# Second experts of an audio tower: routing in three groups instead of two, a new order of the stage, and the last chunk in halves

## The chip, the cores and the metric

The kernel runs on one core of a Trainium2 chip. The engines are TensorE (PE: matrix products and transposes; its weight loads are shown as PEld), VectorE (DVE), ScalarE (ACT), GpSimd (POOL) and SyncE (SP, which here issues transfers). Each works off its own list of instructions in the order written, and they wait for one another with semaphores. The metric is the device time of one execution in microseconds (us).

## The reference, cut to what matters

Sixteen signals are turned into 16 x 255 tokens of 64 numbers. Two blocks of attention and experts follow, each added to its input after a normalisation over the 64 numbers. The change is in the last step, the second layer of experts. Each token's eight router logits choose two of eight experts, with a softmax over the two:

```python
def _moe(tokens, router_w, w1, b1, w2, b2):
    logits = tokens @ router_w.T
    probs = jax.nn.softmax(logits, axis=-1)
    rw, re = jax.lax.top_k(probs, 2)
    rw = rw / jnp.maximum(rw.sum(-1, keepdims=True), 1e-12)
    combine = zeros((N, E)).at[arange(N)[:, None], re].set(rw)
    out = tokens
    for e in range(8):
        h = gelu(tokens @ w1[e] + b1[e])     # 64 -> 64, the exact gelu
        y = h @ w2[e] + b2[e]                # 64 -> 64
        out = out + combine[:, e:e + 1] * y
    return out

h = h + attention1(layernorm(h))
h = h + _moe(layernorm(h), ...)              # what this text is about
```

All experts are computed for all tokens, and the weights, zero for six of eight, are applied to the hidden values.

## The kernel before

The 32 tiles of 128 tokens are worked on in 8 chunks of 4 tiles (CH, TC); 16 signals make two tiles each. The last stage begins while the second attention is still finishing its last signals: `slot(B // 2, k, ...)` and `slot(B // 2 + 1, k, ...)` are those remnants, and on DVE they hold the reading of the turned outputs (slot 3, L2176 to L2187), the last addition of the projected outputs Y (slot 7, L2187, semaphore `s_fin`), and the normalisation of the last signals (L447 to L455 on DVE, the root L460 on POOL, the scaling L472 on DVE).

For a chunk c the stage does this, in columns of 512 tokens:

- PE turns the normalised tokens (`x_turn`, L1821), and ACT copies them out (`columns_out`, L2067).
- PE multiplies with the router (`logits`, L1837); DVE copies the logits (`logits_out`, L2266) and finds the two best (`rank`, L2271 and L2274).
- For 16 tiles at once, DVE takes the difference of the two best (`difference`, L2279 and L2280), ACT its exponential (`gap`, L2072), and DVE builds the weights of the eight experts, split into three bf16 parts (`combine`, L2285 to L2304).
- PE turns these weights (`weights`, L1847), and ACT copies them out (L2076).
- For each of two groups g of four experts: PE's `hidden(c, g)` (L1861), ACT's gelu (L2097), PE's `spread(c, g)` of the weights over the rows (L1874), DVE's `weigh(c, g)` (L2322), PE's `second(c, g)` (L1884, with the bias L1889 where g is 0).
- ACT copies the chunk's sum (`y_out`, L2082), PE turns it (`sum_turn`, L1899), and DVE adds its two halves to the tokens (`finish`, L2312 and L2313). POOL has added the normalised tokens to them before (`add_x`, L2458). SP stores the chunk with four transfers, in a loop over the chunks (`store`, L2476).

Each engine's order is written out by hand. The work shares PE's eight result banks: the hidden values have banks 0 to 3, the spread weights 4 and 5, the sums bank 6, the turned sums bank 7; tokens, logits and turned weights borrow banks between. Bank 6 also holds the attention's projected outputs Y. A reader must be done with a bank before the next result is written there, and most of the waits say that. `keep_clock` is a filler: products of constants that nobody reads. On ACT, Exp and Gelu lie in different tables, so that a `gap` between two gelus costs a load of each (ACT_TABLE_LOAD).

DVE's `combine(n)` works on half of the tiles (`half`), and it stands behind `best(0)` to `best(3)` for the first half and between two weighings of chunk 2 for the second.

Of the kernel before, what the change touches and what calls it, by code (L numbers as in the profile page):

```python
# [25 lines left out]
P = 128  # L26
# [61 lines left out]
def tower(nc, x, taps, consts, w_raw, gate_b0, w1_01, b1_0, w2_0, b2_0, gamma,  # L88
          split_sel, wpos, wproj, bproj, b1_1, w2_1, b2_1, out):
    with ExitStack() as ctx:  # L90
# [1379 lines left out]
        def attention1_and_experts1(block, e0):  # L1470
# [66 lines left out]
            half = NT // 2  # L1537
# [7 lines left out]
            wgt = [mo[:, 2048 + 512 * n:2560 + 512 * n] for n in range(4)]  # L1545
            y_sb = mo[:, 4096:4608]
            yy = mo[:, 4608:4864].rearrange("p (t d) -> p t d", t=TC)
            GROUPS = 2
            X_BANK, WEIGHT_BANK = (0, 1, 0, 1, 7, 7, 7, 7), (7, 6, 4, 5)
            LOGIT_BANK = (2, 4, 2, 4, 4, 4)  # L1550
            def logit_tile(c, k):
                bank, column = (LOGIT_BANK[c] + k % 2, k // 2) if c < 6 else (7, k)
                return ps[:, bank, E * column:E * column + E]

            def logit_tiles(c):
                if c < 6:
                    both = ps[:, LOGIT_BANK[c]:LOGIT_BANK[c] + 2, 0:TC // 2 * E]
                    return both.rearrange("p n (t e) -> p t n e", t=TC // 2)[:, :, :, 0:E]
                return ps[:, 7, 0:TC * E].rearrange("p (t n e) -> p t n e", n=2, t=TC // 2)[:, :, :, 0:E]

            H1, CB, Y1, YT = (lambda g, n: ps[:, 2 * g + n]), (lambda n: ps[:, 4 + n]), ps[:, 6], ps[:, 7]
            turned_weights = lambda d: ps[0:96, WEIGHT_BANK[d // 2], 256 * (d % 2):256 * (d % 2) + 256].bitcast(BF16)
# [12 lines left out]
            def _(pe):  # L1575
# [230 lines left out]
                def x_turn(c):  # L1806
# [3 lines left out]
                    elif c < 4:  # L1810
                        pe.wait_ge(s_xc, c - 1)
                    elif c == 4:
                        pe.wait_ge(s_otr, B)
                    elif c == 5:
                        pe.wait_ge(s_xc, 5)
                    elif c == 6:
                        pe.wait_ge(s_ct, 2)
                    else:
                        pe.wait_ge(s_lc, c)
# [4 lines left out]
                def logits(c):  # L1824
                    pe.wait_ge(s_xc, c + 1)
                    if c == 0:
                        pe.wait_ge(s_E, UNITS)
                    elif c == 1:
                        pe.wait_ge(s_O, QUADS * B)
                        pe.wait_ge(s_k, UNITS)  # L1830
                    elif c < 4:
                        pe.wait_ge(s_lc, c - 1)
                    elif c < 6:
                        pe.wait_ge(s_lc, c)
                    for k in range(TC):
                        rows = head(k % 2) if c < 6 else head(0)
# [3 lines left out]
                def weights(d):  # L1840
                    pe.wait_ge(s_c3, d // 4 + 1)
                    if d == 0:
                        pe.wait_ge(s_xc, 6)
                    elif d == 1:
                        pe.wait_ge(s_ct, 1)
# [4 lines left out]
                def hidden(c, g):  # L1850

                    s = GROUPS * c + g
                    if s == 0:
                        pe.wait_ge(s_xc, 4)
                    elif s == 1:
                        pe.wait_ge(s_lc, 3)
                    else:
                        pe.wait_ge(s_hid, s - 1)
# [5 lines left out]
                def spread(c, g):  # L1864

                    s = GROUPS * c + g
                    pe.wait_ge(s_ct, 1 if s < 2 else 4 if s < 7 else CH)
                    if s == 0:
                        pe.wait_ge(s_lc, 6)
                    if s >= 1:  # L1870
# [6 lines left out]
                def second(c, g):  # L1877

                    s = GROUPS * c + g
                    if g == 0 and c >= 1:  # L1880
                        pe.wait_ge(s_ysb, c)
                    pe.wait_ge(s_wgt, s + 1)
                    for n in range(2):
# [8 lines left out]
                def sum_turn(c):  # L1892
# [3 lines left out]
                    else:  # L1896
                        pe.wait_ge(s_lc, CH)
                    for k in range(TC):
# [7 lines left out]
                slot(B // 2, 3, ("tail",))  # L1906
                x_turn(2)
                logits(1)
                x_turn(3)
                logits(2)  # L1910
                logits(3)
                hidden(0, 0)
                slot(B // 2, 6, ("tail",))
                x_turn(4)
                hidden(0, 1)
                logits(4)
                x_turn(5)
                slot(B // 2, 7, ("tail",))
                pe.wait_ge(s_lc, 5)
                keep_clock(5, 2)  # L1920
                logits(5)
                weights(0)
# [672 lines left out]
```

## Time and profile before

| | before |
|---|---|
| median of 3 runs | 729.52 us (726.92 to 729.8) |
| the profiled execution | 728.98 us |
| its span, first to last instruction | 727.2 us |
| PE, DVE, ACT, POOL busy in the span | 87%, 79%, 69%, 48% |
| mean granted clock of PE | 0.968 of 2.4 GHz |

The span is what the trace shows; the execution's own time has 1.78 us around it. Views used below: the chain of waits (the work that ended last, followed back step by step), the timeline of an engine (instructions in order of time, neighbours of one kind merged), the windows (busy time of each engine in a stretch, with the granted clock), the figures of one line, and the issues of transfers. Times of day are microseconds from the start of the span. A matrix product's shown duration is longer than the distance to the next one, since they overlap in the array.

### The profile page before, as it was taken

The numbers are of one execution on the slowest core, as the hardware profiler recorded it, in microseconds if no ns is written. First come the engines' busy times: TensorE is split into PE (matmuls) and PEld (weight loads), VectorE is DVE, ScalarE is ACT, GpSimd is POOL, SyncE is SP. The second block draws the span as 40 slices with busy tenths as digits, with TensorE's granted clock in tenths as the row PEclk, the third lists the DMA queues.
The fourth block names the chain that finished last, engine by engine and source line by source line (L and its number), as shares of the span: only waits on it lengthen the run. The fifth ranks groups of instructions, "written<-read, shape, count | busy, mean of one in ns | idle before, by whom it ended". The sixth has DMA issues, their size and how long they took to land.

```text
span 727.2 us, 16349 instructions
## 1 busy us (share of the span) xinstructions
PE 631.7 (87%) x4940; PEld 347.4 (48%) x4940; DVE 571.1 (79%) x1627; ACT 501.2 (69%) x1264; POOL 351.6 (48%) x440
## 2 busy tenths in 40 slices
PE   5548998999999997999999998699898889877895
PEld 4534665566666664222222225355565555554331
DVE  6676786777777776789999989659888888959753
ACT  2746875888888874567777777648777777755552
POOL 1006577778878775523444444725354555423000
PEclk9858999999999999999999999799999999998999
DMA  4030000000000000633333330000000000000011
GB/s 112 1 116 1 1 3 0 0 0 0 0 0 0 0 1 3 205 118 119 117 117 114 108 117 16 2 0 2 2 1 0 0 0 0 1 1 1 11 23 27
DMA packets 22422, 24.37 MB, mean 34 GB/s; under 512 B 12390, under 2 KB 13414, under 8 KB 22118
## 3 DMA queue, kind: packets, MB, share of 16 engines
q1 hardware_dynamic: 20135, 23.31, 10.3%
q10 hardware_dynamic: 2239, 0.49, 0.3%
q8 instruction: 22, 0.36, 0.2%
q14 instruction: 26, 0.21, 0.1%
HBM read 22.48 MB, written 1.31 MB: 33 GB/s over the span
## 4 chain that ended last, share of the span: by engine, by line
PE 51%; DVE 25%; issue 9%; ACT 3%; POOL 2%; DMA 2%; SPq 0%; DVEq 0%; POOLq 0%; ACTq 0%
PE ps L726 8%; PE ps L762 8%; DVE big L1110 6%; PE ps L1591 5%; PE ps L1613 4%; PE ps L720 4%; DVE big L2130 3%; DVE big L1151 3%; PE ps L1597 2%; DVE big L1060 2%; PE ps L712 2%; PE ps L1884 2%; PE ps L708 2%; PE ps L1861 2%; PE ps L1728 1%
## 5 line engine op out<-in xcount | busy, mean ns | idle before, releaser
L1367 POOL TENSOR_TENSOR big<-big 128x1024 f32<-128x1024 f32 x64 | 119.8, 1893 | 47.0 <-DVE big L1171 47.0
L949 ACT ACTIVATE big<-ps,big 128x255 f32<-128x255 f32 x256 | 117.0, 483 | 10.0 <-DVE big L1165 7.5
L911 ACT ACTIVATE big<-ps,b1s 128x512 f32<-128x512 f32 x128 | 80.7, 682 | 29.4 <-PE ps L644 28.3
L1165 DVE TENSOR_REDUCE big<-ps 128x4 f32<-128x1020 f32 x64 | 75.1, 1213 | 26.0 <-PE ps L720 26.0
L1988 ACT ACTIVATE big<-ps 128x1024 f32<-128x1024 f32 x64 | 65.9, 1030 | 33.1 <-PE ps L1603 30.8
L726 PE MATMUL ps<-cst,big 128*128 128x128 f32 x512 | 78.3, 287 | 7.0 <-POOL big L1367 3.0
L2130 DVE TENSOR_REDUCE big<-ps 128x4 f32<-128x1020 f32 x64 | 78.1, 1220 | 6.8 <-DVE res L2187 2.5
L1177 DVE COPY mid<-ps 128x512 f32<-128x512 f32 x96 | 63.5, 686 | 19.0 <-PE ps L726 15.7
L726 PEld LDWEIGHTS ps<-cst,big 128*128 128x128 f32 x512 | 55.5, 143 | 41.5 <-issue 20.8
L644 PE MATMUL ps<-big,wall 64*128 64x512 f32 x256 | 72.1, 640 | 0.4 <-ACT big L882 0.4
L655 PE MATMUL ps<-big,w2s 128*64 128x512 f32 x256 | 69.0, 616 | 2.6 <-DVE big L1151 2.2
L762 PE MATMUL ps<-mid,big 128*64 128x256 f32 (+1 forms) x512 | 69.9, 393 | 0.0
L1151 DVE SCALAR_TENSOR_TENSOR big<-ps,b2s,mid 128x512 f32<-128x512 f32 x64 | 48.0, 749 | 10.3 <-DMA mid<-spread_w 6.8
L949 ACT ACTIVATION_READ_ACCUMULATOR big<-ps,big 128x1 f32 x256 | 55.6, 217 | 0.0
L1591 PE MATMUL ps<-big,selqk 128*128 128x256 bf16 x384 | 52.8, 273 | 0.7 <-ACT big L1964 0.4
L465 POOL TENSOR_TENSOR big<-big 128x4 f32<-128x4 f32 x16 | 16.4, 1028 | 65.0 <-DVE big L455 64.9
L1110 DVE TENSOR_TENSOR big<-big 128x512 f32<-128x512 f32 x56 | 47.1, 841 | 0.0
L937 ACT ACTIVATE big<-ps 128x512 f32<-128x512 f32 x64 | 34.9, 602 | 12.6 <-PE ps L708 10.4
L460 POOL TENSOR_TENSOR mid<-mid 128x2 f32<-128x2 f32 x16 | 11.5, 716 | 61.7 <-DVE mid L455 61.7
L1591 PEld LDWEIGHTS ps<-big,selqk 128*128 128x128 bf16 x384 | 32.7, 97 | 17.1 <-issue 13.5
L1597 PE MATMUL ps<-big 64*128 64x256 bf16 x256 | 25.4, 273 | 17.8 <-DVE big L2130 17.7
L762 PEld LDWEIGHTS ps<-mid,big 128*64 128x64 f32 (+1 forms) x512 | 31.3, 137 | 19.0 <-issue 8.4
(282 smaller groups left out, 1317.7 us busy)
## 6 DMA issues: line engine op xcount, KB each, us to landing
mid<-spread_w SPq DMA_DIRECT2D x128, 128.0 KB, 2.8
mid<-in_split_sel SPq DMA_DIRECT2D x1, 1536.0 KB, 7.5
wall<-in_w SPq DMA_DIRECT2D x1, 1280.0 KB, 6.7
out_tokens<-res SPq DMA_DIRECT2D x16, 56.0 KB, 1.6
cst<-in_consts SPq DMA_DIRECT2D x1, 520.5 KB, 5.0
pexp<-in_w_raw SPq DMA_DIRECT2D x1, 512.0 KB, 5.5
w2s<-in_w SPq DMA_DIRECT2D x1, 512.0 KB, 3.3
mid<-in_taps ACTq DMA_DIRECT2D x1, 320.0 KB, 3.9
```

The lines of the kernel that those rows point to most:

```text
L644: last = nc.tensor.matmul(H1(e, j), wst[0][half, f:f + P], xc[q][half], start=True, stop=True)
L655: last = nc.tensor.matmul(Y(e)[D * j:D * j + D], w2s[0][:, 2 * e + j], hid[e % 2][j], start=True, stop=True)
L726: last = nc.tensor.transpose(AT[:, j, c, P * tq:P * tq + P], e_sb[r % 4][:, j, tq, P * c:P * c + P], ident)
L762: last = nc.tensor.matmul(O[D * j:D * j + D, par], val[par][0:n, c, D * h:D * h + D], a_sb[r % 4][0:n, j, c], start=(g == 0 and a == 0 and ...
L911: last = nc.scalar.activation(hid[e % 2][j], H1(e, j), ACT.Relu, bias=b1s[0][:, 2 * e + j:2 * e + j + 1])
L949: last = nc.scalar.activation(e_sb[r % 4][:, jj, tq, 0:NW], S[:, 2 * (r % 2) + jj, tq, 0:NW], ACT.Exp, scale=-1.0, bias=minus[r % 4][:, jj ...
L1110: ins = nc.vector.tensor_tensor(acc[q], acc[q], part[e % 2], ALU.add)
L1151: nc.vector.scalar_tensor_tensor(out=acc[q] if e == 0 else part[e % 2], in0=Y(e), scalar=b2s[:, e:e + 1], in1=cb[e % RING], op0=ALU.add, o ...
L1165: nc.vector.tensor_reduce(minus[r % 4], S[:, 2 * a:2 * a + 2, :, 0:NW], AX.X, ALU.min).then_inc(s_mx, 1)
L1367: nc.gpsimd.tensor_tensor(e_sb[r % 4], e_sb[r % 4], bc(inverse[r % 4].unsqueeze(3), [P, 2, 2, 256]), ALU.mult).then_inc(s_A, 1)
L1591: last = nc.tensor.matmul(out_, selqk[:, 2 * p + n, part], parts[par][:, part], start=(part == 0), stop=(part == 2))
L2130: nc.vector.tensor_reduce(mx[k % 2], S[:, :, :, 0:NW], AX.X, ALU.max).then_inc(s_max, 1)
```

## The change

The diff, with the waits shortened to those that the text speaks of. The routing groups are now chunk 0, chunks 1 to 3 and chunks 4 to 7 (`ROUTED`), the logits are copied for chunk 0, chunks 1 to 3, 4 and 5, 6 and 7 (`LOGITS_READ`). Results lie in other banks. POOL adds the tokens of chunk c only when the sum of chunk c - 1 is turned. In the last chunk the second product, `y_out`, the turn and `finish` are done for each of the two signals; SP issues four of its stores, after its loop, and ACT four.

```diff
-            half = NT // 2
-            X_BANK, WEIGHT_BANK = (0, 1, 0, 1, 7, 7, 7, 7), (7, 6, 4, 5)
-            LOGIT_BANK = (2, 4, 2, 4, 4, 4)
+            ROUTED = ((0, 1), (1, 4), (4, CH))
+            LOGITS_READ = ((0, 1), (1, 4), (4, 6), (6, CH))
+            X_BANK, WEIGHT_BANK = (0, 1, 4, 5, 7, 7, 7, 7), (4, 7, 6, 6, 7, 7, 7, 7)
+            YL, YTL = (ps[:, 6, 0:256], ps[:, 0, 0:256]), (ps[:, 7, 0:256], ps[:, 1, 0:256])
...
                 def logits(c):
-                    pe.wait_ge(s_xc, c + 1)
+                    pe.wait_ge(s_xc, c + 1 if c < 4 else c // 2 * 2 + 2)
-                        rows = head(k % 2) if c < 6 else head(0)
+                        rows = head(k % 2) if c < 4 else head(0)
...
                 def weights(d):
-                    pe.wait_ge(s_c3, d // 4 + 1)
+                    pe.wait_ge(s_c3, 1 if d == 0 else 2 if d < 4 else 3)
...
+                    elif d == 4:
+                        pe.wait_ge(s_done, 2)
+                    elif d == 6:
+                        pe.wait_ge(s_ct, 6)
+                        pe.wait_ge(s_done, 3)
...
                 def second(c, g):
+                    if s == 0:
+                        pe.wait_ge(s_fin, B)
+                    elif g == 0:
                         pe.wait_ge(s_ysb, c)
+                    if s == GROUPS:
+                        pe.wait_ge(s_ct, 4)
                     pe.wait_ge(s_wgt, s + 1)
+                    if c == CH - 1:
+                        for b in range(2):
+                            for n in range(2):
+                                last = nc.tensor.matmul(YL[b][D * n:D * n + D], w2s[1][:, 2 * g + n], wgt[2 * g + n][:, 256 * b:256 * b + 256], start=(g == 0), stop=(g == GROUPS - 1))
...
                 def sum_turn(c):
...
+                    elif c == 2:
+                        pe.wait_ge(s_ct, 6)
+                    elif c == 3:
+                        pe.wait_ge(s_ct, CH)
...
 # PE, from slot(B // 2, 3) on
-                x_turn(2); logits(1); x_turn(3); logits(2); logits(3)
-                hidden(0, 0); slot(B // 2, 6, ("tail",)); x_turn(4)
-                hidden(0, 1); logits(4); x_turn(5)
-                slot(B // 2, 7, ("tail",))
-                pe.wait_ge(s_lc, 5); keep_clock(5, 2)
-                logits(5); weights(0)
-                for c in range(CH): ...     # as printed above
+                logits(1); x_turn(2); x_turn(3); hidden(0, 0)
+                logits(2); logits(3); weights(0); hidden(0, 1); spread(0, 0)
+                slot(B // 2, 6, ("tail",)); x_turn(4); hidden(1, 0)
+                slot(B // 2, 7, ("tail",)); spread(0, 1); second(0, 0)
+                x_turn(5); hidden(1, 1); logits(4); logits(5); second(0, 1)
+                pe.wait_ge(s_wgt, 2); keep_clock(4, 3)
+                for d in range(1, 4): weights(d)
+                spread(1, 0); hidden(2, 0); sum_turn(0); spread(1, 1)
+                second(1, 0); hidden(2, 1); x_turn(6); spread(2, 0)
+                second(1, 1); x_turn(7); hidden(3, 0); logits(6); logits(7)
+                spread(2, 1); sum_turn(1); second(2, 0)
+                for c in range(3, CH):
+                    hidden(c, 1); spread(c, 0); second(c - 1, 1)
+                    if c < CH - 1: hidden(c + 1, 0)
+                    spread(c, 1)
+                    if c < 5:
+                        second(c, 0)
+                        for d in (4, 5) if c == 3 else (6, 7): weights(d)
+                        sum_turn(c - 1)
+                    else:
+                        sum_turn(c - 1); second(c, 0)
+                second(CH - 1, 1)
+                for b in range(2): ...      # the two halves of the last sum turned
 # ACT
+                columns_out(0); columns_out(1); gap(0); columns_out(2); columns_out(3)
+                gelu(0, 0); weights(0); gelu(0, 1); slot(B // 2, 6, ())
+                columns_out(4); gelu(1, 0); columns_out(5); gap(1); y_out(0); gelu(1, 1)
+                for d in range(1, 4): weights(d)
+                gelu(2, 0); gelu(2, 1); columns_out(6); y_out(1); columns_out(7)
+                gelu(3, 0); gap(2); y_out(2); gelu(3, 1); weights(4); weights(5)
+                gelu(4, 0); y_out(3); gelu(4, 1); weights(6); weights(7)
+                for c in range(5, CH): gelu(c, 0); y_out(c - 1); gelu(c, 1)
...
+                    for first, n in ((0, 112), (112, 15)):
+                        nc.scalar.dma_start(out[2 * CH - 2 + b, P + first:P + first + n], res[first:first + n, 4 * CH - 4 + 2 * b + 1]).then_inc(s_out, 16)
 # DVE, from slot(B // 2, 1) on
+                logits_out(0); rank(0); difference(0); combine(0)
+                logits_out(1); slot(B // 2, 3, ()); rank(1); weigh(0, 0)
+                rank(2); rank(3); difference(1); slot(B // 2, 7, ()); weigh(0, 1)
+                logits_out(2); combine(1); slot(B // 2, 2, ()); slot(B // 2, 5, ())
+                slot(B // 2, 6, ()); slot(B // 2 + 1, 1, ()); weigh(1, 0)
+                slot(B // 2 + 1, 2, ()); finish(0); rank(4); weigh(1, 1)
+                rank(5); weigh(2, 0); logits_out(3); weigh(2, 1); finish(1)
+                rank(6); rank(7); difference(2); weigh(3, 0); combine(2)
+                weigh(3, 1); finish(2)
+                for c in range(4, CH): weigh(c, 0); weigh(c, 1); finish(c - 1)
+                for b in range(2): ...      # finish of the two halves
 # POOL
-                for c in range(CH - 2): add_x(c)
+                pool.wait_ge(s_c3, 1); add_x(0)
                 norm.root(pool, B - 2); norm.root(pool, B - 1)
-                for c in range(CH - 2, CH): add_x(c)
+                for c in range(1, CH):
+                    pool.wait_ge(s_yt, c); add_x(c)
 # SP
-                with sp.Fori(0, CH) as c:
+                with sp.Fori(0, CH - 1) as c:
                     store(c)
+                for b in range(2):
+                    sp.wait_ge(s_done, CH + b)
+                    for first, n in ((0, 112), (112, 16)):
+                        sp.dma_start(out[2 * CH - 2 + b, first:first + n], res[first:first + n, 4 * CH - 4 + 2 * b]).then_inc(s_out, 16)
```

In `combine` the first comparison and the first product no longer wait for their own end before the next instruction.

## Rows read from the trace of the kernel before

**Rows 1.** The chain of waits: start, us, what.

```profile
656.06 0.20 DVE mid L2266
...
657.37 0.20 DVE mid L2266
...
667.77 2.01 PE ps L1861 x4
...
672.89 0.79 PE ps L1837 x8
...
695.71 1.06 PE ps L1861 x4
696.76 0.32 PE ps L1874 x2
```

**Rows 2.** Timeline of PE: start, us, what, idle time before and what ended it.

```profile
651.07 0.61 PE L1837 MATMUL ps<-gates,big 64*128 64x8 f32 x8 [0.25 <-ACT big L2067]
...
701.11 1.13 PE L1861 MATMUL ps<-big,wall 64*128 64x512 f32 x4
...
706.59 1.13 PE L1861 MATMUL ps<-big,wall 64*128 64x512 f32 x4
...
717.69 1.08 PE L1884 MATMUL ps<-big,w2s 128*64 128x512 f32 x4 [0.56 <-DVE big L2322]
```

**Rows 3.** Windows: stretch, length, busy of PE, PEld, DVE, ACT, POOL, PE's clock, DMA.

```profile
663.00:666.40 3.40, 1.49 (x12) 0.75 (x11) 2.88 (x14) 1.21 (x3) 0.19 (x1) 0.50 0.00 0
685.00:687.00 2.00, 0.28 (x4) 0.26 (x4) 1.82 (x6) 1.99 (x4) 0.00 (x0) 1.00 0.00 0
694.00:705.20 11.20, 11.20 (x55) 3.69 (x56) 6.65 (x12) 6.33 (x12) 0.00 (x0) 1.00 0.12 25
```

**Rows 4.** Timeline of DVE.

```profile
655.03 0.26 DVE L2176 RECIPROCAL big<-ps 128x16 f32<-128x16 f32 x1
...
664.66 0.60 DVE L472 TENSOR_SCALAR big<-res,mid 128x128 f32<-128x128 f32 x2
...
665.97 0.16 DVE L455 TENSOR_TENSOR mid<-mid 128x2 f32<-128x2 f32 x1
666.44 1.29 DVE L2322 TENSOR_TENSOR big<-big,ps 128x512 f32<-128x512 f32 x2 [0.31 <-PE ps L1874]
...
682.28 0.61 DVE L2285 TENSOR_TENSOR mid<-cst,mid 128x128 f32<-128x128 f32 x2
684.22 0.17 DVE L2290 TENSOR_SCALAR mid<-mid 128x16 f32<-128x16 f32 x1 [1.32 <-ACT mid L2072]
...
687.02 0.56 DVE L2304 TENSOR_TENSOR mid<-mid 128x384 bf16<-128x384 f32 x1
```

**Rows 5.** Timeline of POOL.

```profile
656.32 4.14 POOL L2458 TENSOR_TENSOR res<-res,big 128x256 f32<-128x256 f32 x6
666.21 0.71 POOL L460 TENSOR_TENSOR mid<-mid 128x2 f32<-128x2 f32 x1 [5.75 <-DVE mid L455]
```

**Rows 6.** Timeline of ACT and of the transfers that it issues (ACTq).

```profile
1.91 1.84 ACTq L229 DMA_DIRECT2D mid<-in_x  x1
...
676.12 2.42 ACT L2097 ACTIVATE big<-ps,b1s 128x512 f32<-128x512 f32 x4
...
682.61 1.28 ACT L2072 ACT_TABLE_LOAD   x1
683.90 0.22 ACT L2072 ACTIVATE mid<-mid 128x16 f32<-128x16 f32 x1
```

**Rows 7.** Line 2280: count, shortest, median and longest in ns, first and last start.

```profile
L2280 DVE CAST mid<-mid x2: 173/462/751, 659.1 to 678.9; 128x32 f32<-128x32 uint32 x2
```

**Rows 8.** Timeline of the transfers that SP issues.

```profile
44.90 0.90 SPq L1442 DMA_DIRECT2D w2s<-in_w  x2
...
721.31 2.43 SPq L2476 DMA_DIRECT2D out_tokens<-res  x4
```

**Rows 9.** Line 2476, the stores, in the form of rows 7.

```profile
L2476 SPq DMA_DIRECT2D out_tokens<-res x32: 322/332/1232, 681.4 to 724.1; - x32
```

More of the change, by code:

```diff
@@ new lines, in _ @@
+                pe.wait_ge(s_wgt, 2)
+                keep_clock(4, 3)
+                for d in range(1, 4):
+                    weights(d)
+                spread(1, 0)
+                hidden(2, 0)
+                sum_turn(0)
+                spread(1, 1)
+                second(1, 0)
+                hidden(2, 1)
+                x_turn(6)
+                spread(2, 0)
+                second(1, 1)
+                x_turn(7)
+                hidden(3, 0)
+                logits(6)
+                logits(7)
@@ L2115, in _ @@
-                y_out(CH - 1)
+                gelu(1, 0)
+                columns_out(5)
+                gap(1)
+                y_out(0)
+                gelu(1, 1)
+                for d in range(1, 4):
+                    weights(d)
+                gelu(2, 0)
+                gelu(2, 1)
+                columns_out(6)
+                y_out(1)
+                columns_out(7)
+                gelu(3, 0)
+                gap(2)
+                y_out(2)
+                gelu(3, 1)
+                for d in (4, 5):
+                    weights(d)
@@ new lines, in _ @@
+                gelu(4, 0)
+                y_out(3)
+                gelu(4, 1)
+                for d in (6, 7):
+                    weights(d)
+                for c in range(5, CH):
+                    gelu(c, 0)
+                    y_out(c - 1)
+                    gelu(c, 1)
+                act.wait_ge(s_yt, CH - 1)
+                for b in range(2):
+                    act.wait_ge(s_w2, GROUPS * CH + b)
+                    nc.scalar.activation(y_sb[:, 256 * b:256 * b + 256], YL[b], ACT.Copy).then_inc(s_ysb, 1)
@@ L2345, in _ @@
+                slot(B // 2 + 1, 2, ())
+                finish(0)
                 rank(4)
[L2346 to L2347 removed]
+                weigh(1, 1)
                 rank(5)
[L2349 to L2355 removed]
+                weigh(2, 0)
+                logits_out(3)
+                weigh(2, 1)
@@ L2356, in _ @@
+                finish(1)
+                rank(6)
+                rank(7)
+                difference(2)
+                weigh(3, 0)
+                combine(2)
+                weigh(3, 1)
+                finish(2)
+                for c in range(4, CH):
                     weigh(c, 0)
-                    if c == 2:
-                        combine(1)
                     weigh(c, 1)
                     finish(c - 1)
-                finish(CH - 1)
+                dve.wait_ge(s_with_x, CH)
```

252 lines of the change are left out of this document (124 added, 128 removed).

## Prediction

> **What bounds the kernel now.** I read the page first: TensorE (PE) is busy for 87% of the span, VectorE (DVE) for 79%, ScalarE (ACT) for 69%. The change touches only the last tenth, from 650 us on, so I then read the chain of waits there and the timelines beside it. Up to 664 us the chain runs on DVE: copies of logits, ranking, and the routing weights of 16 tiles built at once [rows 1, 4]. From 694 on it runs on PE: from the second hidden product of chunk 5 to that of chunk 6 it takes 706.59 - 701.11 = 5.48 us, and of the 11.2 us from 694.0 PE is busy for 11.20 [rows 2, 3]. Between them PE waits for weights, tables and weighed tiles, and from 663.0 its granted clock is 0.50 (1.2 GHz), after waits that left it busy for 1.49 of 3.4 us [rows 3]. In the tail, PE's last second product starts at 717.69, the last store is issued at 724.1, and the span ends at 727.2 [rows 2, 9].
>
> With PE saturated from chunk 4 on, the change gains only if PE waits less before that, or in the tail.
>
> **The change, by a walk through the new orders.** I lay each engine's new order down with the durations of these rows, from the end of the first logits (651.07 + 0.61 = 651.7), which nothing new precedes [rows 2].
>
> *Prices.* DVE: logits copy and ranking of a chunk 657.37 - 656.06 = 1.31, the copy 0.23 of it; the reading of the attention's last outputs (slot 3) 656.06 - 655.03 = 1.03 [rows 1, 4]. Weighing two tiles 1.28, of which the next instruction overlaps 0.08; scaling a pair of tiles and the statistics of the next 665.97 + 0.16 - 664.66 = 1.47, POOL's root between them 0.71 [rows 4, 5]. A finish has two instructions over half of a weigh's elements, 0.8. A combine of 16 tiles: 687.02 + 0.56 - 682.28 less the 1.32 for ACT = 3.98, and 3.85 without one of its links [rows 4]. There is none of 4 or 12 tiles in the trace. Its 16-element instruction takes 0.17, its 128-element ones 0.3; twelve at the former price are 2.1, so both lie between 2.1 and 3.9, and scaled by elements I take 2.6 and 3.4. PE: hidden 1.06, spread 0.32, logits from one half of the rows 0.79 [rows 1]. What a chunk's 5.48 has besides two of each is 2.7: second products 1.01, with the bias 1.12, and the sum's turn 0.59; turning tokens is the same work, and four small weight turns are half of it at most. ACT: gelu of two tiles 1.2, a table load 1.28, columns, y or weights out 0.5 to 0.6, less than gelu's 0.6 each [rows 6].
>
> *First group.* DVE: copy, rank, difference (0.3), combine of 4 tiles: 651.7 + 0.25 + 1.07 + 0.32 + 2.6 = 655.95, so chunk 0 is weighed from 658.6 on instead of 666.44 [rows 4]. Then the price. DVE goes on with the copy of chunks 1 to 3 (0.55 with its wait), slot 3 (1.03), rank 1 (1.07), weigh (1.2), rank 2 and 3 (2.15), difference (0.35) and only then slot 7 (0.3), which reads Y: 655.95 + 6.65 = 662.6. The first second product needs that read, because it writes Y's bank. PE is through everything ahead of it at 660.5 and waits 2.1 us. From 662.65 PE does second 1.12, tokens 0.59, hidden 1.06 and two logits 1.58: 667.0. DVE is done weighing at 663.9, but its next instruction is the copy of those logits, with the whole combine of chunks 1 to 3 queued behind it: it idles 3.1 us. Copy and combine end at 667.1 + 0.25 + 3.4 = 670.75. The keep-clock products cover 1.6 of PE's wait for it, 1.2 stay open.
>
> *Weighing chunk 1* stands behind the last two normalisations: 2 x 1.47 + 0.71 + 0.15 of handing over = 3.8, so it ends at 675.85. PE reaches the spread that needs it at 673.8 and waits 2.05. Scaling 0.64, finish 0.8, rank 4 1.07, weigh 1.28 on DVE give 679.6 (PE waits 0.65), then on ACT gelu 1.2 and columns 0.6, on PE the last tokens turned (0.6, wait 0.5), hidden, and logits 6 and 7 (1.58): 684.7.
>
> *Third group.* DVE, idle since 681.8, copies these logits and does weigh 1.2, finish 0.8, rank 6 and 7 2.15, difference 0.35, weigh 1.2, combine of 16 tiles 3.85: 685.1 + 9.55 = 694.65. PE waits 0.75 for the weigh in it and from 692.4 for the combine, 2.3 us. Turning chunks 4 and 5 (0.6) and ACT's two copies (1.1) come next, and the sum's turn waits for the copies, since all share one bank: 1.2 more. It is done at 697.05. The next pass has 6.0 us of PE work and the same wait for chunks 6 and 7 (1.2): chunk 5's second hidden product starts at 704.25. Before it was 701.11 [rows 2]. All that follows has the old order, so the walk loses 3.1 us to here. The waits that I count come to 12.2 us.
>
> *Adding tokens chunk by chunk.* POOL's six adds from 656.32 to 660.46 fell on DVE's first cast, 0.751 us against 0.173 for the second group's [rows 5, 7]. My walk has the short values already, so what the move gives is in it. Each late add of 0.7 is ready a chunk ahead: nothing; at worst it delays a finish by 0.7, in the slack that DVE has beside PE's 5.48.
>
> *Tables.* One more gap of the logits means two more table loads, 5 instead of 3. Each is 1.28, and the next ACTIVATE follows 0.01 after it (682.61 + 1.28, 683.90) [rows 6]. One ends on the path: gelu of chunk 1 waits behind it and ends at 671.25, with the weights of chunk 1 turned at 671.1. The Trainium skill ("ScalarE: Activation LUTs", What ACT_TABLE_LOAD costs) adds a drain of 1380 ns to each load, 2.66 us for a switch; by that the walk would lose 1.4 us more. The trace shows no such drain.
>
> *Tail.* Second product, y, turn and add go by halves, and DVE ends earlier. But that is hidden: SP is still issuing chunk 6 until 721.65, 3.96 after the start of the last second product [rows 2, 8]. SP then has four issues as before (ACT has the other four). Without the loop they follow each other by 0.47 (two in 0.90) instead of 0.55, and without the loop's turn: the last at 721.9 + 1.4 = 723.3, against 724.1. Gain 0.75. If chunk 6's one long issue (1.232, the median is 0.332) is gone too, 1.65; if ACT's four each take the longest there is, 1.84, the last starts at 717.69 + 2.1 + 5.5 = 725.3, a loss of 1.2 [rows 6, 8, 9]. I take -0.75.
>
> *Clock.* The new waits of 2.1, 2.05 and 2.3 + 1.2 us leave PE as open as what went before the halved clock. A fall costs where PE has work: hidden 2.01 instead of 1.06 [rows 1], and in the same ratio a spread 0.25 and half of a second product 0.5: 1.7. I count one, behind the longest wait (692.4 to 696.45).
>
> Sum: 3.1 - 0.75 + 1.7 = +4.05 us. The profiled execution took 728.98 for a span of 727.2; the median of the runs is 729.52. The forecast is 728.98 + 4.05 = **733.0**.
>
> **Rivals.**
> *No fall of the clock:* 731.3. For it: PE kept its clock through 685 to 687, where it was busy for only 0.28 of 2 us [rows 3]. Against it: the new wait is longer.
> *A fall behind all three waits:* 731.3 + 5.1 = 736.4. Against it: a fall behind the wait for chunk 1's weighing is partly eaten by the next wait.
> *Not slower, the third group hidden:* if the weights of chunks 4 to 7 are there when PE has done chunk 3's second product (692.4), the waits of 2.3, 1.2 and 1.2 go, and 731.3 - 4.7 = 726.6. For it: the old kernel's combine of the same tiles began at 682.28 [rows 4]. It decides whether DVE's 9.55 us from 685.1 shrink or start 2.3 us earlier, which needs the logits of chunks 6 and 7 by 682.4; against it, four waits in a row stand ahead of them.
> *Stores on two queues cost:* ACT's issues at 1.84: 733.0 + 2 = 735.0.
>
> **Numbers.** Chances: forecast 0.35, no fall 0.22, several falls 0.20, third group hidden 0.18, stores 0.05. About 0.5% (3.6 us) is what a measurement here can tell from no change: from 725.9 to 733.2 counts as the same. Just under half of the forecast (0.17) and the case without fall (0.20 of its 0.22) fall under that upper bound, and half of the hidden group (0.09) above the lower; with 0.01 of the falls, that is 0.47. Slower: 0.18 + 0.02 + 0.19 + 0.05 = 0.44. Faster: the other half of the hidden group, with the tail's 1.65 and short combines, 0.09. The range goes from the hidden group, 726.6, to 738.0, three falls with a tail that gains nothing and DVE 0.8 behind. The forecast's own range is 731 to 735.
>
> **What would show it.** Right: the first weights done near 656; PE waiting about 2 us for DVE's add of Y ahead of the first second product; DVE idle for some 3 us ahead of the copies of logits 4, 5 and of 6, 7; PE waiting for the last combine near 693; chunk 5's second hidden product near 704 to 706; the stores' end half a microsecond to one closer to the last second product. Wrong: if that hidden product starts before 701, one of DVE's four waits is not there.

## The result, and the profile after

The changed kernel takes 732.18 us (median of 7 runs, 729.5 to 733.6), the kernel before 729.29 (7 runs, 726.89 to 732.84): a ratio of 1.0052, 95% interval 1.0029 to 1.0074. The medians differ by 2.9 us, and the interval leaves out 1, so the change is slower. The ratios here and below leave out executions in a slower state (one of the kernel before in a later series, 1014.5 us) and need not be the quotient of two medians (here 1.0040). The forecast was 733.0, with a range of 726.6 to 738.0. The profiled execution took 731.64 us for a span of 729.8, before 728.98 for 727.2. PE's share stayed at 87%, its mean clock at 0.968.

The last stage began 0.94 us earlier in this execution (first logits at 650.13 instead of 651.07 [rows 2]), with the same code ahead of it. So everything below is also given from the start of the first logits (written +).

PE's timeline after, the rows where the walk had put its anchors and its waits (start, us, what, idle time before and what ended it); L1836 are logits, L1908 second products, L1854 turned weights, L1882 spread, L1929 the sum's turn, L1869 hidden products:

```profile
650.13 0.62 PE L1836 MATMUL ps<-gates,big 64*128 64x8 f32 x8 [0.25 <-ACT big L2112]
...
661.50 1.47 PE L1908 MATMUL ps<-big,w2s 128*64 128x512 f32 x4 [1.66 <-DVE res L2255]
...
665.76 1.85 PE L1836 MATMUL ps<-gates,big 64*128 64x8 f32 x16
...
671.22 0.87 PE L1854 MATMUL ps<-ident_b,mid 128*96 128x128 bf16 x12 [1.12 <-DVE mid L2374]
...
676.22 0.39 PE L1882 MATMUL ps<-big,selb 24*128 24x512 bf16 x2 [1.82 <-DVE big L2392]
...
683.35 1.84 PE L1836 MATMUL ps<-gates,big 64*128 64x8 f32 x16
...
695.61 0.65 PE L1854 MATMUL ps<-ident_b,mid 128*96 128x128 bf16 x8 [1.71 <-DVE mid L2374]
697.52 0.63 PE L1929 MATMUL ps<-cst,big 128*128 128x128 f32 x4 [1.26 <-ACT big L2121]
...
704.87 0.63 PE L1929 MATMUL ps<-cst,big 128*128 128x128 f32 x4 [1.26 <-ACT big L2121]
705.43 1.13 PE L1869 MATMUL ps<-big,wall 64*128 64x512 f32 x4
```

Read it by the brackets. Nearly all of the waits that the walk counted are there, on the engine and line that it named: 1.66 for DVE's addition of Y (L2255), 1.12 for the second combine (L2374), 1.82 for chunk 1's weighing (L2392), 1.71 for the third combine, 1.26 twice for ACT's copies. Only the 0.75 for a weighing in the third group is missing. The last row is chunk 5's second hidden product: +55.30, before +50.04 (701.11 [rows 2]), so 5.26 us late.

DVE's timeline after shows where these waits come from:

```profile
654.60 0.26 DVE L2374 TENSOR_TENSOR mid<-mid 128x96 bf16<-128x96 f32 x1
655.13 0.26 DVE L2335 COPY mid<-ps 128x96 f32<-128x96 f32 x1 [0.28 <-PE ps L1836]
...
661.16 0.29 DVE L2255 TENSOR_TENSOR res<-res,ps 128x128 f32<-128x128 f32 x1
661.48 1.28 DVE L2392 TENSOR_TENSOR big<-big,ps 128x512 f32<-128x512 f32 x2
667.71 0.23 DVE L2335 COPY mid<-ps 128x64 f32<-128x64 f32 x1 [4.94 <-PE ps L1836]
667.85 0.41 DVE L2355 TENSOR_TENSOR mid<-cst,mid 128x96 f32<-128x96 f32 x2
...
670.71 0.46 DVE L2374 TENSOR_TENSOR mid<-mid 128x288 bf16<-128x288 f32 x1
...
685.30 0.22 DVE L2335 COPY mid<-ps 128x64 f32<-128x64 f32 x1 [3.18 <-PE ps L1836]
...
690.60 1.29 DVE L2392 TENSOR_TENSOR big<-big,ps 128x512 f32<-128x512 f32 x2 [0.55 <-PE ps L1882]
...
695.00 0.56 DVE L2374 TENSOR_TENSOR mid<-mid 128x384 bf16<-128x384 f32 x1
```

The first weights are done at 654.86 (+4.73), and PE turns them 8.5 us earlier than before, from the first logits. But DVE reads slot 7 only 6.3 us later, and it idles 4.94 us ahead of a copy of logits, with the whole combine (L2355 to L2374) queued behind it. Not all of that idle time is the order of DVE: the combine's last input, ACT's exponential, is there only at 666.39 (666.18 + 0.21, in the rows on tables below), since ACT does it behind the columns of chunk 5.

The windows after (columns as in rows 3): the first wait, the two stretches of half clock, and the third group:

```profile
656.00:661.50 5.50, 3.45 (x19) 1.31 (x15) 5.11 (x44) 3.96 (x8) 1.13 (x2) 1.00 0.00 0
662.06:665.46 3.40, 3.40 (x14) 1.54 (x11) 0.70 (x2) 1.17 (x2) 0.00 (x0) 0.50 0.02 5
...
685.95:689.35 3.40, 3.40 (x12) 1.15 (x12) 3.26 (x24) 0.18 (x1) 0.72 (x1) 0.50 0.09 18
692.40:705.20 12.80, 8.57 (x55) 3.47 (x54) 7.49 (x18) 7.74 (x14) 0.73 (x1) 1.00 0.05 11
```

PE's granted clock is 0.50 (1.2 GHz) twice, and PE is busy for all of both stretches, so both halve real work. The first follows the wait for slot 7; the second begins behind the two chunks' 8-column logits that started at 683.35, with the waits of 1.82, 0.61 and 0.45 us further ahead. In the third group, where PE was busy for 11.20 of 11.2 us before [rows 3], it is busy for 8.57 of 12.8, at full clock.

The stores after: the transfers by engine (SPq and ACTq issue them), then SP's line in its loop (count, shortest, median, longest in ns):

```profile
717.49 7.57 SPq L2558 DMA_DIRECT2D out_tokens<-res  x8
725.28 1.76 SPq L2566 DMA_DIRECT2D out_tokens<-res  x4
```

```profile
724.40 1.77 ACTq L2183 DMA_DIRECT2D out_tokens<-res  x4
```

```profile
L2558 SPq DMA_DIRECT2D out_tokens<-res x28: 322/331/379, 677.8 to 724.7; - x28
```

From the start of the last second product to the end of the span it is 7.84 us, before 9.52 (from 717.69 [rows 2]). But the one issue of 1.232 [rows 9] is missing here, the longest in the loop is 0.379.

### The profile page after: what moved, and what is told of

The parts are those of the page before. It is cut to its first block, busy times and chain, and to the rows that moved or that the text cites. A ratio compares the mean times of both kernels' runs of the same rounds, so it can differ in the third digit from the quotient of the medians.

```text
span 729.8 us, 16403 instructions
## 1 busy us (share of the span) xinstructions
PE 635.3 (87%) x4952; PEld 351.0 (48%) x4952; DVE 570.9 (78%) x1639; ACT 504.0 (69%) x1268; POOL 351.7 (48%) x440
## 4 chain that ended last, share of the span: by engine, by line
PE 51%; DVE 26%; issue 9%; ACT 3%; POOL 2%; DMA 2%; SPq 0%; DVEq 0%; POOLq 0%; ACTq 0%
PE ps L726 8%; PE ps L762 8%; DVE big L1110 6%; PE ps L1596 5%; PE ps L1618 4%; PE ps L720 4%; DVE big L2198 3%; DVE big L1151 3%; PE ps L1602 2%; DVE big L1060 2%; PE ps L708 2%; PE ps L712 2%; PE ps L1869 2%; PE ps L1733 1%; PE ps L1908 1%
## 5 line engine op out<-in xcount | busy, mean ns | idle before, releaser
L937 ACT ACTIVATE big<-ps 128x512 f32<-128x512 f32 x64 | 34.9, 602 | 11.2 <-PE ps L708 10.2
```

## The experiments

The theory: the change gains early, and DVE's order gives it back, in waits that PE had not had. The rivals: the tail's gain is smaller or larger than it looks; the clock, not the order, is what costs; the late adds cost. The table gives for each kernel the starts of chunk 3's first and chunk 5's second hidden product and the end of the span, from the first logits; the tail from the start of the last second product; the stretches of half clock in the stage (start, length; those that begin behind PE's last product are left out); and the ratio to the kernel before. Positions are of one profiled execution each, ratios of many.

| kernel | hidden(3,0) | hidden(5,1) | end | tail | half clock | ratio (95%) |
|---|---|---|---|---|---|---|
| before | 30.81 | 50.04 | 76.15 | 9.52 | 11.9, 6.8 | 1 |
| after | 32.26 | 55.30 | 79.72 | 7.84 | 12.0, 3.4; 35.8, 3.4 | 1.0052 (1.0029 to 1.0074) |
| t_tail_alone | 30.93 | 51.15 | 75.57 | 7.83 | 12.1, 6.8; 36.0, 6.8 | 0.9981 (0.9964 to 0.9997) |
| t_no_tail | 32.27 | 55.31 | 80.51 | 8.62 | 11.9, 3.4; 35.8, 3.4 | 1.0073 (1.0045 to 1.0100) |
| t_slot7_early | 29.29 | 54.80 | 80.45 | 9.07 | 32.5, 3.4; 42.7, 6.8 | 1.0052 (1.0030 to 1.0073) |
| t_combine_first | 30.26 | 55.31 | 80.99 | 9.09 | 12.4, 3.4; 43.1, 6.8 | 1.0045 (1.0023 to 1.0068) |
| u_late_adds | 31.90 | 53.19 | 78.38 | 8.61 | 11.6, 10.2; 39.0, 6.8 | 0.9993 (0.9970 to 1.0016) |
| u_fillers | 30.67 | 53.20 | 77.62 | 7.84 | none | 1.0019 (1.0001 to 1.0037) |
| u_mended_order | 24.94 | 51.37 | 75.80 | 7.84 | 37.2, 10.2 | 0.9995 (0.9975 to 1.0016) |
| v_mended_fill | 24.93 | 47.98 | 72.39 | 7.83 | none | 0.9956 (0.9939 to 0.9973) |
| u_old_order_best | 32.05 | 50.87 | 76.32 | 8.86 | 12.0, 10.2; 39.3, 3.4 | 0.9956 (0.9938 to 0.9974) |
| v_old_order_fill | 28.10 | 47.23 | 71.65 | 7.83 | 35.9, 3.4 | 0.9927 (0.9907 to 0.9947) |

**t_tail_alone** is the kernel before with the change's last chunk in halves and its stores on two queues; **t_no_tail** the changed kernel without these.

```diff
 # t_tail_alone: these, and second, y_out, sum_turn and finish of the last chunk in halves
-                with sp.Fori(0, CH) as c:
+                with sp.Fori(0, CH - 1) as c:
                     store(c)
-                sp.wait_ge(s_out, 16 * 4 * CH)
+                for b in range(2):
+                    sp.wait_ge(s_done, CH + b)
+                    for first, n in ((0, 112), (112, 16)):
+                        sp.dma_start(...)
 # t_no_tail: the same, with - and + exchanged
```

> The kernel before with the change's tail alone (last chunk in halves, its stores on SP and ACT). Theory (routing and order lose about 5 us, the tail gives 1.7): 1.0 to 1.8 us faster than the kernel before, ratio 0.9975 to 0.9986; the last second product to the end of the span 7.8 us instead of 9.5. Rival (the tail gives nothing, its shorter end in the one profile is the missing long store issue, which is chance): within 0.5 us of before, ratio 1.000, 9.0 us or more from the last second product to the end.

> The changed kernel with the old tail (last chunk whole, all its stores in SP's loop). Theory: 1.0 to 1.8 us slower than the changed kernel, so 4.2 to 5.0 us slower than the kernel before, ratio 1.0058 to 1.0069. Rival (the order costs little and the tail gives nothing): ratio 1.004 to 1.005, as the changed kernel.

The tail alone is 0.9981, so about 1.4 us faster, and the change without it 1.0073, so 2.1 thousandths or 1.5 us worse than with it. Both intervals are wider than the gain itself, and 1.0073 is a little over the range expected. By the profiles, the old tail is 8.62 long without a long issue and 9.52 with one, the new one 7.84 and 9.07 to 9.09. The pair without one gives a gain of 0.78. The other pair gives 0.45, but its long issues are not alike: 1.23 in the old tail, 1.56 and 1.61 in the new ones. A gain of some 0.8, then, and the profile's 1.7 is made of 0.8 and of a long issue that was there before and not after. The long issue is no property of the loop. In the kernel t_combine_first it falls on the four stores behind the loop, which take 3.01 instead of 1.76 us (timeline of SP's transfers; one of ACT's four issues beside it takes 1.57 there):

```profile
716.04 7.56 SPq L2558 DMA_DIRECT2D out_tokens<-res  x8
723.82 3.01 SPq L2566 DMA_DIRECT2D out_tokens<-res  x4
```

**t_slot7_early** moves DVE's addition of Y ahead of one ranking; **t_combine_first** builds the weights of chunks 1 to 3 before it copies the logits of 4 and 5, and ACT takes the second gap before the columns of chunk 5.

```diff
 # t_slot7_early, DVE
                 rank(2)
+                slot(B // 2, 7, ())
                 rank(3)
                 difference(1)
-                slot(B // 2, 7, ())
 # t_combine_first, ACT and DVE
-                columns_out(5)
                 gap(1)
+                columns_out(5)
...
-                logits_out(2)
                 combine(1)
+                logits_out(2)
```

> The changed kernel, but DVE adds the attention's last outputs (slot 7) between rank 2 and rank 3 instead of behind rank 3 and the difference. Theory (the first second product waits for that add, and the logits, the combine and all else of chunks 1 to 3 wait for the product): PE's wait of 1.66 us ahead of the first second product falls to 0.3 to 0.6, the clock's fall behind it goes in part, and the run is 1.3 to 3.0 us faster than the changed kernel: ratio to before 1.001 to 1.0035. Rival (PE's wait there is hidden by the wait for the combine, or by the wait for chunk 1's weighing behind the normalisations): 0 to 0.4 us, ratio 1.0045 to 1.005.

> The changed kernel, but DVE does the combine of chunks 1 to 3 before it copies the logits of chunks 4 and 5, and ACT does that group's exponential before it copies out the columns of chunk 5. Theory (DVE's 3 to 5 us of idle time ahead of the copy delay the normalisations and the weighing of chunk 1): the combine ends near 667 instead of 671.2, the weighing of chunk 1 starts near 672.8, then held by the spread, and the run is 1.5 to 2.2 us faster than the changed kernel: ratio to before 1.002 to 1.0035. Rival (the place is held by ACT's gelu of chunk 1 behind two table loads, and PE's later waits take the gain back): 0 to 0.5 us, ratio 1.0045 to 1.005.

PE's wait ahead of the first second product in t_slot7_early (timeline of PE, then a window):

```profile
658.73 1.08 PE L1908 MATMUL ps<-big,w2s 128*64 128x512 f32 x4 [0.27 <-DVE res L2255]
```

```profile
691.50:698.30 6.80, 5.54 (x21) 1.98 (x18) 2.92 (x6) 2.23 (x4) 0.72 (x1) 0.50 0.09 20
```

The wait shrinks from 1.66 to 0.27 and the half clock behind it is gone (the one behind the logits of chunks 6 and 7 stays), and chunk 3 starts 3.0 us earlier. Yet only 0.5 is left at hidden(5,1), since the clock now falls for 6.8 us behind the wait for the third combine, which the changed kernel had passed at full clock. The other kernel repeats it: 2.0 us earlier at chunk 3, none at hidden(5,1), with a wait of 2.07 for the third combine and half clock behind it (timeline of PE, t_combine_first):

```profile
691.63 0.99 PE L1854 MATMUL ps<-ident_b,mid 128*96 128x128 bf16 x8 [2.07 <-DVE mid L2374]
...
693.88 1.09 PE L1929 MATMUL ps<-cst,big 128*128 128x128 f32 x4 [1.26 <-ACT big L2121]
```

Their ratios can't be told from the change's. So each of the two orders costs what the walk says where it stands, and nothing by itself at the end: the next wait, and the clock behind it, take the gain.

**u_fillers** keeps the changed orders and puts filler products into three waits, for slot 7, for chunk 1's weighing and for the third combine. **u_late_adds** is the kernel before with POOL's adds chunk by chunk, the change's part that was costed at nothing.

```diff
 # u_fillers, PE
                 spread(0, 1)
+                pe.wait_ge(s_hid, 2)
+                keep_clock(2, 3)
                 second(0, 0)
...
                 sum_turn(0)
+                pe.wait_ge(s_ct, 4)
+                keep_clock(6, 3)
                 spread(1, 1)
...
+                        if c == 3:
+                            pe.wait_ge(s_done, 2)
+                            keep_clock(7, 3)
                         for d in (4, 5) if c == 3 else (6, 7):
                             weights(d)
 # u_late_adds, POOL
-                for c in range(CH - 2):
-                    add_x(c)
+                pool.wait_ge(s_c3, 1)
+                add_x(0)
                 norm.root(pool, B - 2)
                 norm.root(pool, B - 1)
-                for c in range(CH - 2, CH):
+                for c in range(1, CH):
+                    pool.wait_ge(s_yt, c)
                     add_x(c)
```

> The changed kernel with three more keep-clock products in each of three waits of PE (ahead of the first second product, of chunk 1's second spread, and of the turning of chunk 4's weights), each as long as the wait at most. Theory (the waits stay and some of the falls of the clock behind them go): no fall within 13 us of the first logits, 0.8 to 2.0 us faster than the changed kernel, ratio to before 1.0025 to 1.004. Rival (the falls lie where the logits of chunks 6 and 7 run, or are of no account, since DVE is the path): 0 to 0.5 us, ratio 1.0045 to 1.0055.

> The kernel before with POOL's adds of the tokens moved as the change moves them, and nothing else. Theory (POOL's adds lengthen DVE's difference, cast and first comparisons by 1.5 us, and DVE is the path there): the first combine ends 1.3 to 1.6 us earlier after the first logits, and the run is 0.8 to 1.6 us faster, ratio 0.998 to 0.999. Rival (PE would wait for something else then): cast back at 0.17 us, but 0 to 0.3 us, ratio 1.000.

With the fillers no stretch of the stage is at half clock (windows of u_fillers; PE's clock is the third number from the end; then two rows of PE's timeline, the logits of chunks 6 and 7, and chunk 3's second spread, which waits for the weighing of its first):

```profile
661.00:671.00 10.00, 8.61 (x58) 5.14 (x54) 5.46 (x23) 6.68 (x10) 0.68 (x1) 1.00 0.01 2
685.00:696.00 11.00, 8.52 (x47) 3.61 (x44) 8.98 (x45) 5.48 (x9) 0.59 (x1) 1.00 0.06 13
```

```profile
681.05 1.84 PE L1836 MATMUL ps<-gates,big 64*128 64x8 f32 x16
...
689.21 0.39 PE L1882 MATMUL ps<-big,selb 24*128 24x512 bf16 x2 [0.65 <-DVE big L2399]
```

hidden(5,1) stands at +53.20, 2.1 earlier, and the ratio falls from 1.0052 to 1.0019. So of the 5.26 us the clock is 2.1, and 3.16 are left: the walk, without the clock, had 3.1. That is the order's loss against the kernel before as it ran, which has 6.8 us of half clock itself (+11.9); against an old order with less of it the loss is larger (v_old_order_fill below, +47.23). The Trainium skill ("TensorE: Matmul & The Clock Gate", Terms) gives half of the throttled time as the penalty at half rate; by that, as an estimate, the two stretches of 3.4 would cost 3.4 us. The trace has 2.1: 1.6 are gained by chunk 3, as half of the first stretch would be, and only 0.5 behind it. There DVE sets the pace, for at full clock PE waits 0.65 for a weighing that the changed kernel does not wait for.

The late adds change nothing that the runs can tell (0.9993). The cast of the first group does get its short time (line 2280 of u_late_adds, in the form of rows 7), and the first weights are turned 1.2 us earlier (+12.09, before +13.31), but the clock is then at half for 10.2 us, where the kernel before had 6.8:

```profile
L2280 DVE CAST mid<-mid x2: 169/172/175, 656.9 to 678.1; 128x32 f32<-128x32 uint32 x2
```

```profile
660.80:671.00 10.20, 9.21 (x40) 4.24 (x40) 8.58 (x49) 4.78 (x9) 2.12 (x3) 0.50 0.01 2
```

The cast beside POOL's adds took 0.751 [rows 7], without them 0.175 at most. The Trainium skill ("SBUF — State Buffer", Who interferes with whom) says that a cast of DVE, in the modes that use both ports, and an instruction of GpSimd lock each other out of a shared port pair, the later one waiting for the whole of the other; this pair agrees, with 0.58 more for the cast and 0.69 for one of POOL's adds (4.14 for six [rows 5]).

**u_mended_order** is the changed kernel with both of the moves above, ACT's gelu of chunk 1 ahead of the sum of chunk 0, chunk 1's weighing between the last two normalisations, and finish and the second weighing ahead of the last scaling; PE's filler at that place is taken out. **v_mended_fill** adds six filler products in the wait for the third combine.

```diff
 # u_mended_order, DVE
                 slot(B // 2, 5, ())
+                weigh(1, 0)
                 slot(B // 2, 6, ())
                 slot(B // 2 + 1, 1, ())
-                weigh(1, 0)
-                slot(B // 2 + 1, 2, ())
                 finish(0)
-                rank(4)
                 weigh(1, 1)
+                slot(B // 2 + 1, 2, ())
+                rank(4)
 # v_mended_fill, PE
+                        if c == 3:
+                            pe.wait_ge(s_done, 2)
+                            keep_clock(7, 6)
                         for d in (4, 5) if c == 3 else (6, 7):
```

> The changed kernel with its DVE orders mended: slot 7 ahead of rank 3, the combine of chunks 1 to 3 ahead of the copy of logits 4 and 5, the weighing of chunk 1 between the last two normalisations, finish 0 and the second weighing ahead of the last scaling and rank 4; on ACT that group's exponential and the gelu of chunk 1 ahead of their neighbours; the filler products are left out. Theory (these orders, not the early start, make the change slow): chunk 3's first hidden product starts 24 to 27 us after the first logits instead of 32.3, chunk 5's second one 47 to 50 instead of 55.3, and the run is 4.5 to 7 us faster than the changed kernel, ratio to before 0.9955 to 0.999. Rival (DVE has too much work whatever the order, because three groups cost it more than two): at most 2 us faster than the changed kernel, ratio 1.002 or more.

> The mended orders, with six filler products (0.27 each) in PE's wait of 2.07 for the last combine. Theory (what is left of the mended orders' gain was eaten by the low clock of 10.2 us that began 1.6 us into that wait, behind which hidden(5,1) came 10.36 after hidden(4,1) instead of some 7): no low clock between hidden(4,1) and hidden(5,1), these two 6.8 to 7.4 apart, hidden(5,1) at +47.8 to +49.0 from the first logits, the ratio to before at 0.991 to 0.997. Rival A (the low clock comes from the waits of 1.26 for the copies of the weights, or from the 8-column products of logits 6 and 7 ahead, which the fillers don't touch): low clock as before them, hidden(5,1) at +51 to +52, ratio 0.998 to 1.001. Rival B (DVE sets the pace there: what PE wins is waited for later): PE's waits grow behind chunk 4 and the ratio is 0.997 to 1.000.

The same stretch, from the wait for the third combine on, in u_mended_order and then in v_mended_fill (windows):

```profile
686.80:697.00 10.20, 8.51 (x26) 3.00 (x26) 3.70 (x7) 3.98 (x7) 0.72 (x1) 0.50 0.07 14
```

```profile
685.00:695.20 10.20, 8.94 (x52) 4.69 (x53) 6.06 (x13) 4.15 (x8) 0.73 (x1) 1.00 0.07 14
```

The mended order brings chunk 3 7.3 us forward against the change, and 3.9 of that reaches hidden(5,1), short of the +47 to +50 expected: from 1.0052 to 0.9995. What is missing goes in the 10.2 us at half clock, in which PE shows 26 products, against 52 with the fillers, a dozen of them the fillers' own. (A filler product is two rows of the trace, so it takes some 0.5 us and not the 0.27 that I had counted: three of them are x6 in 1.56.) Filling the wait gives 3.4 us more at hidden(5,1), and 0.9956. The theory had asked for +47.8 to +49.0 and got +47.98. With order and clock mended, the three groups beat the kernel before, by 0.0044 of 728, 3.2 us. Of these the tail alone gives 1.4 (t_tail_alone), and the kernel before keeps its own half clock.

**u_old_order_best** goes the other way: the old order with the change's tail, the late adds, and ACT's second gap ahead of the sum of chunk 1. **v_old_order_fill** raises the filler before logits 5 from two products to six.

```diff
 # u_old_order_best, ACT (beside tail and late adds)
+                        if g == 0 and c == 2:
+                            gap(1)
                         if g == 0 and c >= 1:
                             y_out(c - 1)
...
-                        if g == 0 and c == 2:
-                            gap(1)
 # v_old_order_fill, PE
-                keep_clock(5, 2)
+                keep_clock(5, 6)
                 logits(5)
```

> The kernel before with the change's tail and late adds, and on ACT the second half's exponential ahead of the copying out of chunk 1's sum, so that its table loads lie in ACT's wait for that sum. Theory: tail 0.8 to 1.5, late adds 0.8 to 1.5, and PE's wait of 1.72 us ahead of chunk 3's second hidden product falls under 0.6: 3.0 to 4.4 us faster than before, ratio 0.994 to 0.996. Rival (the parts hide one another): 1.5 us, the tail's alone, ratio 0.998.

> The old order with the change's tail, late adds and the early second gap, and with four more filler products (0.27 each) in PE's wait of 1.86 for the columns of chunk 5. Theory (the low clock of 10.2 us that began 0.8 behind that wait came of the wait): no low clock before +30 from the first logits, hidden(2,0) at +22 to +23.8 instead of +25.40, but DVE's second combine, not PE, then sets chunk 3, so hidden(5,1) gains 0.5 to 1.5 at most: +49.4 to +50.4, ratio 0.993 to 0.996. Rival (the clock falls for the waits of 0.30 and 0.68 and the short products between them): low clock as it was, ratio as without the fillers, 0.994 to 0.998, hidden(5,1) at +50.9.

u_old_order_best, at 0.9956, lies in the range of its theory: PE's wait ahead of chunk 3's second hidden product falls from 1.72 to 0.19. Its profile is of its slowest execution. First PE's wait for the columns of chunk 5 in it, then the fillers in that wait in v_old_order_fill (timeline of PE):

```profile
660.99 0.61 PE L1838 MATMUL ps<-gates,big 64*128 64x8 f32 x8 [1.86 <-ACT big L2086]
```

```profile
658.95 2.86 PE L1740 MATMUL ps<-cst 128*128 128x256 f32 x12
```

Windows of u_old_order_best and of v_old_order_fill over the 10.2 us from there on:

```profile
661.80:672.00 10.20, 9.40 (x38) 4.19 (x39) 8.21 (x49) 4.42 (x8) 2.12 (x3) 0.50 0.01 2
```

```profile
662.00:672.20 10.20, 9.00 (x64) 4.77 (x64) 9.66 (x59) 5.51 (x10) 2.13 (x3) 1.00 0.01 2
```

Four products more (x12 in 2.86 us, where x4 took 1.13) in a wait of 1.86, and the clock stays at 1.00 through the next 10.2 us. hidden(5,1) gains 3.6 us in the profiles (2.1 us by the ratios), where I had expected 0.5 to 1.5: I had thought that DVE would set the pace of chunks 2 and 3, but the whole stage moved forward. At 723.58 us against 728.02, ratio 0.9927, it is the fastest kernel of the study. So with fillers in both, the two groups in the old order (0.9927, hidden(5,1) at +47.23) are at least as fast as the three in the mended one (0.9956, +47.98); the intervals overlap. That the earlier start pays by itself is not shown.

## Why the prediction was right, and where its terms were off

The sum was +4.05 on the profiled execution. That one shows +2.66 (731.64 less 728.98), which is 5.26 at hidden(5,1), less 1.68 in the tail, less the 0.94 by which the stage began earlier by chance; what is left is rounding. By steps, with the forecast's times shifted to the new start by -0.94:

- **The early start.** First weights done 654.86, forecast 655.0. Combines of 4, 12 and 16 tiles took 2.48, 3.32 and 3.76 us (654.86 - 652.38, 671.17 - 667.85, 695.56 - 691.80), sized at 2.6, 3.4 and 3.85. Right.
- **Slot 7.** PE's wait 1.66 instead of 2.1, its end 661.50 instead of 661.7. Right.
- **The copy ahead of the combine.** The forecast had 3.1 us of idle DVE, it is 4.94. Most of the difference is the clock: hidden and logits between 662.06 and 665.46 ran at half, which I had not put there, and logits 5 were done at 667.61 instead of 666.06. From here to the logits of chunks 6 and 7 all is about 1.2 to 1.6 late.
- **Chunk 1 behind the normalisations.** Wait 1.82, forecast 2.05; then 0.61 and 0.45, forecast 0.65 and 0.5. Right.
- **The third group.** From the copy to the end of the combine it is 10.26 us (695.56 less 685.30), forecast 9.55; 0.55 of the difference is DVE's wait at 690.60 for a spread that PE did late, behind the second stretch of half clock. PE's waits 1.71, 1.26 and 1.26, forecast 2.3, 1.2 and 1.2. Right, but for the 0.75 for a weighing, which shows only at full clock (0.65 in u_fillers).
- **The walk's sum** was 3.1 at hidden(5,1), and u_fillers, without any half clock, has 3.16. This is one execution of each, so the second digit is not to be trusted, but the term stands, as the loss against the kernel before with its own half clock. The waits listed in the walk add up to 11.95, not 12.2; nothing hangs on it.
- **The clock** was mis-placed: one fall of 1.7 behind the wait for the third combine. There were two, behind the first wait and behind logits 6 and 7, together 2.1, and none at the place that I had named. That the size came near is luck: in t_slot7_early and u_mended_order the fall is at my place. The reading that it went out from was wrong too: the 3.4 us in which PE was busy for 1.49 [rows 3] are a part of the halved stretch and not what went before it. Ahead of it lie PE's waits of 0.70 and 1.28 us (660.10 and 662.51 in the kernel before).
- **The tail** gained some 0.8 by the profiles that can be paired, forecast 0.75. The bounds that I gave, -1.65 to +1.2, hold the profile's 1.68 only nearly, since the long issue went and came. ACT's four issues took 0.37 to 0.46 each here, not the 1.84 of the rival; single ones of 0.66 to 1.57 turned up in the three other kernels with a long issue of SP in the new tail.
- **Tables.** Two more loads, 5 instead of 3 in the stage. Behind a load for which the next ACTIVATE waits for nothing else, it starts 0.01 to 0.02 later (timeline of ACT, after):

```profile
664.89 1.28 ACT L2117 ACT_TABLE_LOAD   x1
666.18 0.21 ACT L2117 ACTIVATE mid<-mid 128x12 f32<-128x12 f32 x1
...
692.06 1.28 ACT L2135 ACT_TABLE_LOAD   x1
693.36 1.26 ACT L2135 ACTIVATE big<-ps,b1s 128x512 f32<-128x512 f32 x2
```

So the drain of which the Trainium skill speaks ("ScalarE: Activation LUTs", What ACT_TABLE_LOAD costs) is not in these rows either, and the 1.4 us by that rule did not come.

Of the rivals, "no fall" is what u_fillers makes of the change: 1.0019, some 1.4 us above before, where the rival gave 731.3, 1.8 above the median then shown. "A fall behind all three waits" did not come: the two stretches cost 2.1, not 5.1. "Third group hidden" failed on the condition that it was given: the logits of chunks 6 and 7 were done at 685.2, not by 682.4.

What stays open: why the clock falls behind one wait and not behind another of the same length. The changed kernel passes the wait of 1.71 for the third combine at full clock, t_slot7_early with the same 1.71 does not. The kernel before passes 1.72 and 1.05 us (at 686.75 and 688.92) at full clock and falls behind 0.70 and 1.28. And the stretches of half clock of a single profile needn't be those of the timed runs: u_old_order_best took 727.92 in its profiled execution and 724.82 in the median.

## What to carry to other kernels

An earlier start of one chain is worth what the engine that builds it has left to give: write down, for each consumer of that engine, which instruction it needs and how many stand ahead of it, since work that was ready stood behind work that was not, and PE waited for it. A wait of 1 to 2 us on TensorE is charged twice, once itself and once in the half clock that may follow; a few filler products in it gave back 2.1 to 3.6 us of 730 in three profiles, and 2.1 to 2.8 by the ratios, more than half of what the change itself cost. So compare a new order with the old one after the waits of both are filled. And pair the tails by what single transfers did before crediting a change with them.

## What the runs showed of the hardware that was not expected

- The half clock also began right behind products of 8 columns, issued without a gap (683.35, 16 in 1.84 us), not only right behind a wait. These products alone do not explain it: the same 16 stand in t_combine_first, u_fillers, u_mended_order and v_mended_fill, and the clock holds behind them. The three kernels with the fall (after, t_no_tail, t_slot7_early) have a wait of 1.82 or 1.83 us for chunk 1's weighing ahead of them, which the four others lack.
- The clock turns gains into nothing: 2 to 3 us won at chunk 3 by t_slot7_early and t_combine_first were all but gone at hidden(5,1), each time with a new stretch of 6.8 us of half clock behind the wait for the third combine.
- One transfer issue of 1.2 to 1.6 us, against a median of 0.33, turned up among SP's last stores in four of the twelve profiles: in the loop in the kernel before [rows 9], t_slot7_early (1.56) and u_old_order_best (1.36), and behind it in t_combine_first (1.61). Against the tails without one it is worth 0.9 to 1.25 us of the span (9.52 against 8.62, 9.09 against 7.84).
